# Halves of the last state beside the gates, layer norms moved to VectorE, and a new order of the first loads, in a one-core four-layer mixer

## The reference

```python
x = x + attn_a(LN(x))  # linear attention: q, k through softplus, running sums of k v^T and k
x = x + ffn(LN(x))     # the recurrence below
x = x + attn_b(LN(x))  # causal softmax attention with ALiBi bias, 16 heads of 16
x = x + ffn(LN(x))     # the same weights again

def ffn(x):            # scans over the 8 batches, x_t is one batch: 1024 tokens x 256
    c = broadcast(in_c)
    for x_t in x:
        f = sigmoid(x_t @ wf.T + c @ uf.T + bf)
        i = sigmoid(x_t @ wi.T + c @ ui.T + bi)
        g = tanh(x_t @ wc.T + c @ uc.T + bc)
        c = f * c + i * g
    return tanh(x @ wo.T + c @ uo.T + bo)   # every batch needs the last state c
```

## Time and profile before

| | |
|---|---|
| median of 3 runs | 2955.39 us (2944.89 to 2956.65) |
| the profiled execution | 2952.86 us |
| its span, first to last instruction | 2951.1 us |
| mean granted PE clock | 0.912 |
| busy: PE, DVE, ACT, POOL | 78%, 57%, 43%, 28% of the span |
| the phases | 1 to about 1125 us, 2 from there on |

### The profile page before, as it was taken

How to read it: one execution, slowest core, us unless ns; L and a number is a source line. 1 busy time by engine, 2 the same in 40 slices (tenths; PEclk the granted TensorE clock), 3 DMA queues, 4 the chain that set the end, 5 groups by cost and what they waited for, 6 DMA issues and landing times.

```text
span 2951.1 us, 57293 instructions
## 1 busy us (share of the span) xinstructions
PE 2307.5 (78%) x24195; PEld 1215.9 (41%) x24195; DVE 1677.3 (57%) x3769; ACT 1257.7 (43%) x2023; POOL 826.9 (28%) x692
## 2 busy tenths in 40 slices
PE   1568887888888864188888998889888988898952
PEld 1345555555555542123243443443433434333331
DVE  4346456464564533077576676666766767666225
ACT  1314334333342211035555655555555555555613
POOL 1433232331321014243142242341422413202120
PEclk9779999999999976679899999999999999999986
DMA  3001010010010121122122121230321201203052
GB/s 91 29 16 44 30 44 30 30 44 30 30 37 9 44 65 43 60 89 74 43 89 76 56 87 41 64 102 23 94 71 59 85 18 59 65 25 112 2 200 114
DMA packets 127439, 171.33 MB, mean 58 GB/s; under 512 B 8864, under 2 KB 94880, under 8 KB 127184
## 3 DMA queue, kind: packets, MB, share of 16 engines
q1 hardware_dynamic: 123088, 167.15, 17.3%
q10 hardware_dynamic: 4096, 0.53, 0.1%
HBM read 91.11 MB, written 76.02 MB: 57 GB/s over the span
## 4 chain that ended last, share of the span: by engine, by line
PE 52%; DVE 15%; issue 9%; ACT 9%; DMA 7%; POOL 3%; SPq 3%; ACTq 2%; POOLq 0%; DVEq 0%
PE general L864 8%; PE general L549 8%; DMA k_stacks<-k_stack 6%; PE scores L696 5%; PE out_of_heads L755 5%; DVE maxima L1349 3%; PE general L875 3%; PE general L535 3%; PE general L516 3%; SPq L381 3%; PE scores L672 3%; PE out_of_heads L628 2%; PE turned_scores L710 2%; PE scores L586 2%; PE out_of_heads L638 2%
## 5 line engine op out<-in xcount | busy, mean ns | idle before, releaser
L1349 DVE TENSOR_REDUCE maxima<-scores 128x1 f32<-128x512 f32 (+3 forms) x1536 | 801.1, 553 | 479.2 <-PE scores L672 286.8
L1047 ACT ACTIVATE probs_turned<-turned_scores 128x512 f32<-128x512 f32 x1152 | 684.7, 599 | 660.6 <-PE turned_scores L672 385.8
L696 PE MATMUL scores<-k_stacks,q_stacks 51*128 51x512 bf16 (+3 forms) x1536 | 459.5, 344 | 74.6 <-DVE maxima L1349 35.0
L710 PE MATMUL turned_scores<-q_stacks,k_stacks 53*128 53x512 bf16 (+3 forms) x1536 | 450.6, 337 | 14.2 <-ACT probs_turned L1047 13.8
L696 PEld LDWEIGHTS scores<-k_stacks,q_stacks 51*128 51x128 bf16 x1536 | 128.5, 95 | 325.6 <-DVE maxima L1349 184.3
L672 PE MATMUL scores<-mask_scores,identity 64*128 64x256 bf16 (+3 forms) x954 | 252.0, 264 | 0.0
L672 PE MATMUL turned_scores<-mask_turned,identity 64*128 64x128 bf16 (+3 forms) x969 | 251.3, 259 | 0.0
L1585 POOL TENSOR_SCALAR ln<-x_for_attention,ln_mean_var,ln_rstd 128x256 f32<-128x256 f32 x128 | 158.6, 1250 | 269.1 <-DVEq L1472 135.3
L864 PE MATMUL general<-ln_turned_high,w_high 64*128 64x512 bf16 (+1 forms) x600 | 133.3, 394 | 109.8 <-ACT qk_block L1079 59.3
L1523 POOL TENSOR_TENSOR state_low<-state_doubled,state_high 128x2048 bf16<-128x2048 f32 x16 | 65.1, 4068 | 540.9 <-ACT state_high L995 540.9
L1606 POOL TENSOR_TENSOR ln_low<-ln 128x512 bf16<-128x512 f32 x128 | 133.8, 1053 | 201.6 <-DVE ln L1331 201.6
(11 more groups left out here) (225 smaller groups left out, 5293.6 us busy)
## 6 DMA issues: line engine op xcount, KB each, us to landing
x_after_attention<-x_residual SPq DMA_DIRECT2D x16, 1024.0 KB, 4.5
x_times_wo<-x_wo_out SPq DMA_DIRECT2D x64, 256.0 KB, 2.2
k_stacks<-k_stack SPq DMA_DIRECT2D x64, 212.0 KB
q_stacks<-q_stack SPq DMA_DIRECT2D x64, 204.0 KB
x_for_attention<-in_x SPq DMA_DIRECT2D x8, 1024.0 KB, 5.5
x_residual<-in_x SPq DMA_DIRECT2D x8, 1024.0 KB, 5.5
x_for_attention<-x_after_attention SPq DMA_DIRECT2D x8, 1024.0 KB, 12.2
ffn_h<-x_times_wo SPq DMA_DIRECT2D x32, 256.0 KB, 6.9
```

The source lines that it names most:

```text
L696: mx = pe.matmul(bank_s[:, first * P:(first + tiles) * P], QS[at:at + QROWS, r, i * P:(i + 1) * P], KS[at:at + QROWS, r, k0 * P:(k0 + tile ...
L710: ex = pe.matmul(bank_t[:, first * P:(first + tiles) * P], KS[at:at + KROWS, r, j * P:(j + 1) * P], QS[at:at + KROWS, r, i0 * P:(i0 + tile ...
L1047: nc.scalar.activation(PR[:, s % SLOTS, :], TB[s % 2][:, :], ACT.Exp).then_inc(sem["ex_taken"], 1)
L1349: r = dve.tensor_reduce(MP[:, gg % 2, g, at:at + 1], max_bank[m][:, first * P:(first + tiles) * P], AX.X, ALU.max)
```

## The change

1. **Beginning.** x of batch 0 is loaded ahead of the constants. DVE takes the statistics of batch 0 right after the constants and does its LN itself (POOL keeps `ln_low`); then it splits the two pairs of the first attention's weights. The statistics and LN of batch 1 move up into stage -1, between the first and the second softplus block, and onto DVE. The other four pairs of weights, staged in the unused `attention_out`, and `set_state` follow at step 80 of stage -1, ahead of DVE's first work in stage 0.
2. **Both borders.** After group 1 of the last batch's gates, ACT and DVE convert the first token half of the state, and PE multiplies it 11 steps into the gates of the second half; DVE adds. Only the second half is left behind the gates. `state_low` of both halves is DVE's.
3. **Border of phase 1.** Pieces 0 and 1 of h of batch 0 get sum, tanh and addition beside the gates. LN of batch 0 in phase 2 is DVE's.
4. **SP in stage -1 of phase 2.** Pieces 2 and 3 of h go ahead of group 0, and group 1 behind the q and k stores.
5. **End.** LN of the last batch is DVE's. A half batch of the output is now a half of the tokens; the first four sums, tanhs and the first two additions lie beside the gates, four more sums and additions ahead of the second half's product.

The core of the diff (indentation shortened):

```diff
+def by_vector(phase, which, b):
+    if phase == 1:
+        return which == 2 or b < 2
+    return (which, b) in ((1, 0), (2, B - 1))
...
+        WS = [flat(ON[:, 4 * n:4 * n + 4, :]) for n in range(2)]
...
+    load_x(0)
...
-    load_weights(0, 2, 2)
-    load_x(0)
-    load_weights(8, 4, 0)
-    sp.wait_ge(sem["w_split"], w.next("w_split", 2))
-    sp.wait_ge(sem["const_ready"], w.next("const_ready"))
+    for r in range(2):
+        load_weights(0, r, QK[:, r, :], r)
+    for r in range(2):
+        load_weights(8, r, WS[r], 2 + r)
+    sp.wait_ge(sem["const_ready"], 1)
...
+        if b == -1:
+            for r in (2, 3):
+                sp.wait_ge(sem["w_split"], r + 1)
+                load_weights(8, r, WS[r % 2], 2 + r % 2)
...
-        return t[b].rearrange("(p n) d -> p (n d)", p=P)[:, half * KT * CH:(half + 1) * KT * CH]
+        return t[b][half * CH:(half + 1) * CH].rearrange("(p n) d -> p (n d)", p=P)
...
-        if b == -1:
-            load_group(0)
-            load_group(1)
         if batch_in(b + 2):
             load_h(b + 2, 2)
             load_h(b + 2, 3)
+        if b == -1:
+            load_group(0)
...
+        if b == -1:
+            load_group(1)
...
+    def state_part(half, banks, apart):
         pe.wait_ge(sem["state_split"], w.next("state_split"))
-        for c in range(4):
-            if c >= 2:
-                pe.wait_ge(sem["cu"], w.next("cu"))
-            by_token(G[c % 2], UO, CP, c, apart=apart).then_inc(sem["g_dve"], 1)
-        for c in range(2):
-            pe.wait_ge(sem["cu"], w.next("cu"))
+        for c in (2 * half, 2 * half + 1):
+            by_token(banks(c), UO, CP, c, apart=apart).then_inc(sem["g_dve"], 1)
...
+        if s == B * BATCH + HALF_DONE + 11:
+            state_part(0, lambda c: general_for("dve", "cu"), False)
+    state_part(1, lambda c: general_for("dve", "cu"), False)
     drain_general()
...
+    def bank_of_state(c):
+        bank = take_bank(c % 2, "cu")
+        general_of["dve"].append(bank)
+        return bank
...
+        if s == B * BATCH + HALF_DONE + 11:
+            state_part(0, bank_of_state, True)
+    state_part(1, bank_of_state, True)
...
+    def last_state_high(half):
+        if half:
+            act.wait_ge(sem["gate_used"], w.next("gate_used"))
+        else:
+            act.wait_ge(sem["gate_used"], w.seen["gate_used"] + 1)
+        at = slice(half * CH, (half + 1) * CH)
+        nc.scalar.copy(CP[0][:, :, at], CS[:, :, at]).then_inc(sem["state_high"], 1)
+    def tanh_h(fb, c):
+        act.wait_ge(sem["h_sum"], 4 * fb + c + 1)
+        nc.scalar.activation(XI[:, c % 2, :], XI[:, c % 2, :], ACT.Tanh).then_inc(sem["h_tanh"], 1)
...
+        if s == B * BATCH + HALF_DONE + 1:
+            last_state_high(0)
+        if s in (B * BATCH + HALF_DONE + 25, B * BATCH + HALF_DONE + 27):
+            tanh_h(0, (s - B * BATCH - HALF_DONE - 25) // 2)
+    last_state_high(1)
+    def final_tanh(first, last):
+        for n in range(first, last):
+            act.wait_ge(sem["fin_sum"], n + 1)
+            a = FW[n % B][n // B]
+            nc.scalar.activation(a, a, ACT.Tanh).then_inc(sem["fin_tanh"], 1)
...
+        if s == B * BATCH + HALF_DONE + 1:
+            last_state_high(0)
+        if s == B * BATCH + HALF_DONE + 18:
+            final_tanh(0, 2)
+        if s == B * BATCH + HALF_DONE + 25:
+            final_tanh(2, 4)
+    last_state_high(1)
+    final_tanh(4, 2 * B)
...
+    def last_state_low(phase, half):
+        dve.wait_ge(sem["state_high"], (phase - 1) * (B + 1) + B + half)
+        at = slice(half * CH, (half + 1) * CH)
+        dve.tensor_tensor(CP[1][:, :, at], CS[:, :, at], CP[0][:, :, at], ALU.subtract
+                          ).then_inc(sem["state_split"], 1)
...
-    split_weights(0, 2, 0)
-    split_weights(8, 4, 4)
-    set_state()
...
+    def normalise(which, src, c, phase=1):
         for t in (2 * c, 2 * c + 1):
-            i = dve.tensor_scalar(XN[:, t, :], XR[:, t, :], MV[:, 1, t, 0:1], RS[:, 1, t:t + 1],
+            i = dve.tensor_scalar(XN[:, t, :], src[:, t, :], MV[:, which, t, 0:1], RS[:, which, t:t + 1],
                                   ALU.subtract, ALU.mult)
-        i.then_inc(sem["ln_norm1"], 1)
+        i.then_inc(sem[f"ln_norm{phase}"], 1)
...
+                if k % 2 == 0:
+                    dve.wait_ge(sem["h_added"], 4 * fb + (k - 62) // 2 + 1)
...
+            if k == 77 and by_vector(2, 1, fb):
+                dve.wait_ge(sem["xt_dve"], turned_before(2, "ln1", fb))
+                for c in range(4):
+                    normalise(0, XA, c, 2)
+        if b == B and k == 41:
+            dve.wait_ge(sem["xt_dve"], turned_before(2, "ln2", pb))
+            for c in range(4):
+                normalise(1, XR, c, 2)
...
+            at = k + 56 if fb == 1 else k
+            if 62 <= at < 70:
...
+            if by_vector(1, 1, fb) and at == 77:
+                if turned_before(1, "ln1", fb):
+                    dve.wait_ge(sem["xt_dve"], turned_before(1, "ln1", fb))
+                for c in range(4):
+                    normalise(0, XA, c)
+        if b == -2 and k == 80:
+            split_weights(0, 0, [QK[:, r, :] for r in range(2)], 0)
+        if b == -1 and k == 80:
+            split_weights(8, 4, [WS[r % 2] for r in range(4)], 2)
+            set_state()
...
+        if b == B and k == HALF_DONE + 2:
+            last_state_low(1, 0)
+        if b == B and k == HALF_DONE + 13:
+            state_part(0)
...
+    last_state_low(1, 1)
+    state_part(1)
     set_state()
+    def final_sum(n):
+        b, half = n % B, n // B
+        if half == 0:
+            dve.wait_ge(sem[f"fin_in{b}"], 64)
+        dve.tensor_tensor(FW[b][half], FW[b][half], flat(CU[:, 4 * half:4 * half + 4, :]), ALU.add
+                          ).then_inc(sem["fin_sum"], 1)
+    def final_add(n):
+        b, half = n % B, n // B
+        dve.wait_ge(sem["fin_tanh"], n + 1)
+        dve.tensor_tensor(FX[b][half], FX[b][half], FW[b][half], ALU.add).then_inc(sem["fin_done"], 1)
...
+        if s == B * BATCH + HALF_DONE + 2:
+            last_state_low(2, 0)
+        if s == B * BATCH + HALF_DONE + 14:
+            state_part(0)
+            final_sum(0)
+            final_sum(1)
+        if s == B * BATCH + HALF_DONE + 24:
+            final_sum(2)
+            final_sum(3)
+            final_add(0)
+            final_add(1)
+    for n in range(4, B):
+        final_sum(n)
+        if n == 4:
+            last_state_low(2, 1)
+        final_add(n - 2)
...
-        if (phase, which) != (1, 2):
+        if not by_vector(phase, which, b):
...
+        if fb == 1:
+            layer_norm(1, 1, XA, fb)
...
+        if batch_in(pb) and pb < B - 1:
+            state_low(1, pb)
```

133 lines of the change are left out of this document (55 added, 78 removed).

## The result

The changed kernel takes **2866.23 us** (median of 4 runs, 2864.87 to 2869.3) where the kernel before, run beside it, takes 2956.02 (4 runs, 2944.89 to 2957.64): a ratio of 0.9705, 95% interval 0.968 to 0.9731. The forecast was 2857 with a range of 2838 to 2880, so it is 9 us short, inside the range. The profiled execution took 2869.3 us, span 2867.5; the spans differ by 83.6 us, the medians by 89.8. Steps are compared by the profiled executions and then against the runs.

What follows compares the result with a forecast made beforehand. PE is busy 78% of the span, so gains come only where the pipeline is empty and one chain sets the time. 26 + 14.5 + 32 + 24 = 96.5 off 2952.9 gives 2856.4, stated as 2857, range 2838 to 2880.

Steps and rivals of the forecast that it cites:

- Beginning: Kernel start up to the low copy of stage 0: PE starts at 29.1, copy at 95.4; gain 26 us, bounds 19 and 30.
- Border: Between the phases: less work behind the last gate, start state 8.3 us, LN on DVE; gain 14.5 us, bounds 10 and 18.
- the prediction's other reading: At the border: DVE and POOL exclude each other on the shared port, start state the full 11.3 us, gain 11.5.
- Queue: SP in stage -1 of phase 2: h lands earlier, scores start at 1224 instead of 1255.95; gain 32 us, bounds 25 and 37.
- I cost it at nothing; up to 5 if it is late: Phase 2's first scores: group 1, needed at 1254, was to land at 1250 to 1253, so no wait was charged.
- Rival A: Stack queue gives half: scores at 1240, or, second form, a stall of 16 after 36 steps; 2873 us, chance 0.16.
- End: Last gates to last addition: LN on DVE 7.7, product costs 3.0, tail 32.3 instead of 51.4; gain 24 us, bounds 19 and 27.
- The pipeline between: Stages between the four changed places: assumed to keep their pace, as the diff leaves them alone, so gains add.
- B: Beginning of the kernel gives little, reloads stuck on SP or `phi` 10 late: gain 14 instead of 26, 2868 us, chance 0.14.
- C: Phase 2 stages: SP left one group behind, each of eight stages showing a group's wait; slower, 3067 us, chance 0.03.
- D: Last gates at both borders: a wait in the moved steps holds them, borders give nothing; 58 left, 2895 us, chance 0.04.
- signs of being wrong: Transfer wait behind group 0's scores, PE idle over 1 us in last gates, DVE idle in tail, changed phase 2 stage times.

Runs made afterwards that it cites:

- the run with group 1 next: Changed kernel with group 1's transfers issued right behind group 0's, ahead of the store of x and the q and k stores: 2856.67 us, ratio 0.9669.
- the cut: Changed kernel with every stack transfer of 51 or 53 rows split at row 48: 2800.49 us; the same split on the kernel before: 2886.29 us.
- the one with the later start state: Changed kernel with the start state of phase 2 put behind the layer norm of batch 0 instead of ahead of its statistics: 2866.27 us, ratio 0.9707.

## Why the prediction was right

- **Beginning, 26: measured 25.5.** PE's start (29.1) came at 28.35, the copy (95.4) at 96.14. Two misses cancel in it: the constants were 1.4 late, not 2.5, but between PE's start and the last `phi` some 6.5 us were given back and not 5.2. DVE's weights and state ended 0.7 late, with 1.24 us of waiting for a reload at 81.30.
- **Border, 14.5: measured 12.9.** Statistics came 16.7 us behind the last gate, as forecast, with 8.5 up to the end of the additions (8.4) and 8.3 from there to the statistics (8.3), 7.8 of them the start state and not the 11.3 of the prediction's other reading. Beside POOL's additions one of its passes took 2.49 us, alone 1.42 (88.21 in the beginning); before, three did (2.42, 2.17 and 3.23 instead of 1.43, 1.24 and 2.29). So DVE and POOL do hold each other up here, which is the other reading in kind, and the change leaves less of the state beside POOL. LN gave 7.7. From the residual's statistics to the last gate it took 62.6 us (1041.04 to 1103.6) instead of 60.0, the 2.6 charged for the product. What I had not charged lies ahead of it: the product of the residual ahead of these statistics took 7.16 us instead of 5.41, because PE's clock was down there (single matmuls 0.42 us up to 1036.3 and 0.27 from 1036.8; before, 0.27 throughout). The row can be read at all because phase 1 took the same time in both profiled executions, 943 and 945 us from the low copy of stage 0 to these statistics.
- **Queue, 32: measured 27.** Up to the scores the step was right and a little too careful: 34.2 us, as group 0 took 25.1 us, not 26.4. The step that failed is "I cost it at nothing; up to 5 if it is late": group 1 was issued when forecast (29.2 us behind group 0, forecast 26 to 29), but then needed 32.5 us and not 26, and PE waited 8.20. All of the difference is in its issue: its last transfer was issued 10.9 us behind its first (1187.37 to 1198.25), where in the earlier trace rows it is 4.8, and landed 21.53 us later, as there (21.56). So the queue was still full when SP came to it. Rival A's second form was there, then, at half its price (8.2 for 16); the run with group 1 next took it away. The rate per engine of the Trainium skill (DMA: Bandwidth & Descriptors, Specifications) made the prediction's estimate of 19 us for a group, with a gain of 37; by the prediction's own sum it would be 39 (1255.95 - 1197.72 - 19). The measured 25.1, issues included, decides against it.
- **End, 24: measured 23.4**, in it LN 7.8, the product in the gates 3.6 (3.0 forecast), the tail 32.2 (32.3). The output product ahead of the gates took 5.08 us instead of 4.11 and stands in the row above in the table.
- **The pipeline between**, which the sum took as unchanged, gave back 5.2: 1.0 at the product just named. The waits for stacks there (23.3) are those of before (22.9), so the cause of the other 4.2 is left open. They may be no effect of the change: from the transposes of stage 0 to the last statistics, six kernels with this queue, the changed one among them, needed 1523.9 to 1535.8 us (1531.3 in the changed kernel, 1526.2 before).

Sum of the profiled executions: 25.5 + 12.9 + 27.0 - 5.2 + 23.4 = 83.6, forecast 96.5. By the medians the 13 us between them are 9: the profiled run was the slowest of its four. Rivals B, C and D did not occur. Of the signs of being wrong, two did: the wait for a transfer behind group 0's scores, and a pipeline that took another time than before. That the total is only 9 us off is in part luck, as the spread of phase 1 (last section) is as large.

What the prediction missed altogether is larger than all of this. It named 39 GB/s at a DMA share of 0.11, cited the rule that explains them, and used both only to price a wait, not to ask why a group is slow. What the cut gives was in the earlier trace rows to be seen.

## What to carry to other kernels

When a transfer that the chain waits for runs at a small DMA share, look at its row count before reordering the queue around it: here a transfer of 48 rows and one of the rest in place of one of 51 or 53 gave 73 us to the kernel before, where the whole change gave 90. When a transfer is moved ahead on a queue, follow the next one that now stands behind what was passed, and price it with the queue full, not alone. Pieces moved off an empty stretch of one engine can gain less further on than at the first copy (13.6 us there, about 5 one stage later), so count the first place at which all engines have met again (a store behind the stage), not the first copy.

## What the runs showed that I had not expected

**Phase 1 has a spread of its own.** Between the low copy of stage 0 (94.58 to 96.74) and the end of phase 1, kernels with the same code need different times: SP's store of x ahead of the border is issued at 1028.40, 1029.94 and 1030.16 in three, at 1035.32 in one, and at 1038.37 to 1041.74 in five. These are single executions, and one kernel has both kinds: the one with the later start state took 2855.0 us in the profiled execution, 2865.45 to 2868.6 in the three others. Windows of the first stage, of the changed kernel and then of that one:

```profile
96.00:216.00 120.00, 86.76 (x1132) 62.75 (x1137) 59.43 (x127) 38.17 (x52) 34.42 (x20) 0.82 0.03 10
```

```profile
96.00:216.00 120.00, 85.05 (x1203) 61.21 (x1208) 60.96 (x130) 38.49 (x53) 34.38 (x20) 0.88 0.05 17
```

The granted clock is 0.82 against 0.88, and from 216 to 1028 us 0.95 against 0.96. But the first window does not decide it: the kernel with LN on POOL has 0.88 there too and is at 1039.91. The distance between the two executions shown grows in steps, 2.7 us at the store behind stage 0, 5.1 one stage later, 4.7 four stages after that, 8.3 and 10.9 at the last two. What sets off a step is open. The 10 us are as large as three of the effects tested here, which is why those are read at their places in the trace and not from medians.

**A transfer on few engines blocks SP as well.** In the changed kernel the issue of the store of x behind group 0 took 8.79 us on SP; with the cut at 48, 0.38. So slow groups also delay everything that stands behind them on the list, which is one way in which they can cost more than PE's waits for them (47.2 us) add up to.
